# Reordering one queue's transfers in a four-layer graph network: adjacency load first, next token loads between the way out and the reads back

## The reference

```python
h = relu(layernorm(x)); x = x + L0(h, adj)          # 2-layer graph network, softmax masked by adj
h = relu(layernorm(x)); x = x + L1(h, adj, adj)     # 12-head attention, adj as bias
h = relu(layernorm(x)); x = x + L2(h, adj)          # 12-head attention, adj as bias
h = relu(layernorm(x)); x = x + L3(h, adj)          # 2-layer graph network:
    u = h @ h.T / sqrt(D); a = softmax(u) * adj; attn = a / (sum(a) + 1e-10)
    ctx = (attn*upper) @ (h @ wl.T) + diag(attn) * (h @ ws.T) + (attn*lower) @ (h @ wr.T)
    h = relu((ctx - mean) / sqrt(var + eps) * g + beta)
```

## Time and profile before

| | us |
|---|---|
| median of 3 runs | 2807.22 (2806.8 to 2807.78) |
| the profiled execution | 2810.98 |
| its span, first to last instruction | 2809.2 |
| PE busy in the span | 2684.6 (96%) |
| DVE, POOL, ACT busy | 2184.4, 1495.1, 1224.2 |
| mean granted TensorE clock | 0.988 |

### The profile page before, as it was taken

The page is one execution under the profiler, slowest core; times in us unless marked ns, Lnnn a source line. Parts: engine busy times, 40 slices in busy tenths (PEclk is TensorE's granted clock), DMA queues, the critical chain, the costliest instruction groups (busy, mean ns, idle before and its releaser), DMA issues.

```text
span 2809.2 us, 85451 instructions
## 1 busy us (share of the span) xinstructions
PE 2684.6 (96%) x33582; PEld 2472.3 (88%) x33582; DVE 2184.4 (78%) x4130; ACT 1224.2 (44%) x2007; POOL 1495.1 (53%) x2499
## 2 busy tenths in 40 slices
PE   7999999999988999999989999998999999999997
PEld 7988888888878899999888999998888888888886
DVE  5776777767767788888877888888677777777776
ACT  3333333333333454544544545454444444444443
POOL 2222222223214566665544666665677777777776
PEclk9999999999999999999999999999999999999999
DMA  5332232322323433333353333333132222222221
GB/s 162 103 108 84 84 106 63 113 77 89 103 76 108 142 121 124 125 123 121 108 158 111 121 122 127 121 122 119 55 96 80 71 90 78 71 90 78 72 84 48
DMA packets 224451, 284.59 MB, mean 101 GB/s; under 512 B 18256, under 2 KB 203984, under 8 KB 224336
## 3 DMA queue, kind: packets, MB, share of 16 engines
q1 hardware_dynamic: 224336, 282.96, 32.1%
HBM read 182.62 MB, written 100.27 MB: 101 GB/s over the span
## 4 chain that ended last, share of the span: by engine, by line
PE 37%; issue 22%; DVE 16%; POOL 15%; DMA 5%; ACT 3%; SPq 2%; POOLq 0%; DVEq 0%; ACTq 0%
PE ps L373 27%; POOL wide L1610 7%; PE ps L1435 3%; PE ps L1417 3%; PE ps L1450 2%; DMA adjin<-in_adj 2%; DVE heads L1308 2%; DVE wide L1299 2%; DVE heads L1316 2%; DVE heads L1322 2%; DMA bounce<-xin 1%; POOL small L722 1%; DVE wide L1332 1%; POOL wide L1595 1%; PE ps L1965 1%
## 5 line engine op out<-in xcount | busy, mean ns | idle before, releaser
L373 PE MATMUL ps<-w_hi,split 128*128 128x384 f32 x4608 | 1271.6, 346 | 26.3 <-ACT split L1673 17.6
L373 PEld LDWEIGHTS ps<-w_hi,split 128*128 128x128 f32 x4608 | 849.1, 191 | 56.9 <-issue 17.8
L373 PE MATMUL ps<-split,w_hi 128*128 128x256 f32 x4608 | 863.4, 283 | 14.8 <-DVE w_lo L450 11.1
L373 PE MATMUL ps<-w_lo,split 128*128 128x384 f32 x2304 | 787.6, 342 | 0.0
L373 PEld LDWEIGHTS ps<-split,w_hi 128*128 128x128 f32 x4608 | 721.3, 189 | 32.2 <-ACT w_hi L439 11.3
L373 PE MATMUL ps<-split,w_lo 128*128 128x256 f32 x2304 | 584.7, 283 | 0.0
L373 PEld LDWEIGHTS ps<-split,w_lo 128*128 128x128 f32 x2304 | 435.7, 189 | 17.3 <-issue 17.3
L373 PEld LDWEIGHTS ps<-w_lo,split 128*128 128x128 f32 x2304 | 439.0, 191 | 1.3 <-issue 1.2
L731 POOL TENSOR_TENSOR rstd<-mv,pos_half 128x2 f32<-128x2 f32 x64 | 59.0, 923 | 569.3 <-DVE mv L926 569.3
L1187 POOL TENSOR_TENSOR wide<-wide 128x192 f32<-128x192 f32 x256 | 213.4, 865 | 252.1 <-ACT wide L1253 252.1
L1610 POOL TENSOR_TENSOR wide<-wide,row 128x192 f32<-128x192 f32 x512 | 315.7, 652 | 1.5 <-ACT wide L1686 1.5
(11 more groups left out here) (145 smaller groups left out, 4473.8 us busy)
## 6 DMA issues: line engine op xcount, KB each, us to landing
bounce<-xin SPq DMA_DIRECT2D x127, 384.0 KB, 3.1
wide<-bounce SPq DMA_DIRECT2D x508, 96.0 KB, 2.2
x_after<-wide SPq DMA_DIRECT2D x96, 384.0 KB, 2.5
wide<-x_after SPq DMA_DIRECT2D x96, 384.0 KB, 3.3
xin<-x_after SPq DMA_DIRECT2D x190, 192.0 KB
xin<-in_x SPq DMA_DIRECT2D x66, 192.0 KB
wide<-in_x SPq DMA_DIRECT2D x32, 384.0 KB, 4.4
out<-wide SPq DMA_DIRECT2D x32, 384.0 KB, 2.8
```

The lines of the kernel that those rows point to most:

```text
L373: mm = nc.tensor.matmul(out, t if tokens_stay else w, w if tokens_stay else t, start=(k == 0), stop=(k == len(pairs) - 1))
```

## The change

`swap_quarters` is cut in two: `put_quarters` (wait for the turned group, write it to `bounce`) and `get_quarters` (wait until it has landed, four reads). In `turn(i)` the adjacency load comes before the way out, and the next token loads between the way out and the reads. No other engine's instructions change in kind or in order.

```diff
+    def at_turn(i):
+
         if isinstance(i, int) and i >= ITER:
-            if nxt == len(phases):
-                return
-            now, i = phases[nxt], i - ITER
+            return (phases[nxt] if nxt < len(phases) else None), i - ITER
+        return ph, i
+
+    def put_quarters(s, i):
+        now, i = at_turn(i)
+        if now is None:
+            return
         sp.wait_ge(now.dve_done[s], now.DV[s]("turned", i))
         sp.dma_start(g.bounce[s], g.turned[s][:]).then_inc(now.sems.bounced[s], 16)
+
+    def get_quarters(s, i):
+        now, i = at_turn(i)
+        if now is None:
+            return
         sp.wait_ge(now.sems.bounced[s], 16 * (i + 1))
...
     def turn(i):
         for s in range(STREAMS):
             store_and_reload(s, i - 2)
-            swap_quarters(s, i)
+            adjacency(s, i)
+            put_quarters(s, i)
             tokens(s, i + 1)
-            adjacency(s, i)
+            get_quarters(s, i)
```

More of the change, by code:

```diff
@@ L512, in tokens @@
             sp.dma_start(g.xin[s][:, t], source[i * STREAMS + s][t]).then_inc(now.sems.x_in[s], 16)
-    def swap_quarters(s, i):
-        now = ph
+    def at_turn(i):
         if isinstance(i, int) and i >= ITER:
-            if nxt == len(phases):
-                return
-            now, i = phases[nxt], i - ITER
+            return (phases[nxt] if nxt < len(phases) else None), i - ITER
[4 more added lines that the diff above has]
+            return
         sp.wait_ge(now.dve_done[s], now.DV[s]("turned", i))
         sp.dma_start(g.bounce[s], g.turned[s][:]).then_inc(now.sems.bounced[s], 16)
+    def get_quarters(s, i):
+        now, i = at_turn(i)
+        if now is None:
+            return
         sp.wait_ge(now.sems.bounced[s], 16 * (i + 1))
@@ L525, in swap_quarters @@
             sp.dma_start(now.bufs[s].hT0_rows[rows], g.bounce_quarter[s][k]).then_inc(now.sems.hT_in[s], 16)
+    def swap_quarters(s, i):
+        put_quarters(s, i)
+        get_quarters(s, i)
     def matrix(m):
```

## The result

The changed kernel takes 2837.8 us (median of four runs, 2835.6 to 2843.9) where the kernel before takes 2807.1: a ratio of 1.0112, with a 95% interval of 1.0095 to 1.013. It is 1.1% slower; I had forecast 0.8% faster. The profiled execution took 2835.6 us around a span of 2833.8; the one of before 2811.0 around 2809.2. That is 24.6 us more span.

The account below looks back on a forecast made before the run. PE bounds the kernel, except for its idle time in phase 3 (32.2 us, partly from late adjacency blocks) and at borders. Gains 10.8 + 5 + 2.7 + 2.7 + 1.5 = 22.7 us gave 2784.5 us; forecast 2775 to 2795, 8 in 10: 2773 to 2801.

Parts of the forecast that it names:

- Reads back later: Phase 3, stream 1: reads issued 1.56 us later land at 2224.5; DVE loses under 1 us, PE nothing.
- rival of late reads: Phase 3, stream 1: reads land behind the tokens, PE waits 0.65 us longer per turn, +9.1 us; 2813.9 us; chance 0.09.
- Adjacency load earlier, phase 3: Phase 3: block lands some 6 us earlier, POOL's 25 waits go; gains 10.8 us, plus 5 at L1772.
- the discount on L1772: Phase 3: only 5 us of PE's 7.3 us wait on DVE's L1772 counted, since DVE gets reads back later.
- the first rival: Phase 3: POOL's head start doesn't pay, PE keeps 15.8 us of gaps, only borders' 6.9 us gained; 2800.3 us; chance 0.14.
- PE's wait for ACT's split stays: Phase 3: PE's 12.8 us of waits on ACT's L1673 stay, since POOL itself waits on DVE in that chain.
- Late reads in phase 1 are hidden: Phases 0 and 1: use is 11.7 us behind the reads' start, so 3 to 5 us more are hidden.
- Adjacency at the borders: Borders to phases 1 and 2: 2.7 us gained together; border to phase 3: 1.5 us.
- Tokens earlier at the border to phase 1: Border of phases 0 and 1: tokens leave 1.35 us sooner twice, all of it counting; 2.7 us gained.
- the sum of 22.7 us: All gains, phase 3 and borders together: 10.8 + 5 + 2.7 + 2.7 + 1.5 us.

Follow-up runs that it names:

- number 9: Changed kernel, reads before tokens in: phase 3's stream 1 (0.9947); all phase 3 (0.9942); also phase 2's last two turns (0.9913); ratios to the kernel before.
- Number 1: Changed kernel with the four reads back right behind the way out again, tokens after them, adjacency load still early: 2777.9 us, ratio 0.9899.
- number 4: Changed kernel with each stream's tokens loaded by four DMAs of 32 rows instead of two of outer size 4: 2764.4 us, ratio 0.9845.
- number 7: Order of the kernel before (reads, tokens, adjacency last) with the tokens as four DMAs of 32 rows: 2775.2 us, ratio 0.9873.

## Why the prediction was wrong, point by point

- **Reads back later: the step that failed.** I had a lower bound of 2223.1 and an upper one of 2227.1 for the landing, took 2224.5 "nearer the lower bound since the reads' own row is the nearest kind", and gave the slower rival 0.09. The reads landed at 2228.0, beyond the upper bound. The row of 2.2 us is that of reads with nothing narrow ahead of them; it was not the nearest kind for reads behind tokens. The row that was, the 6.75 us that tokens took at the border, I had used for the bound and set aside. Even the bound that I made of it was 0.9 us too early. I also never asked why 384 KB of tokens need 6.75 us where reads of 96 KB, four in a row, land 2.2 us behind their issue: single microseconds of the trace of before show the tail at 0.26.
- **The rival of late reads** had the right mechanism and place (stream 1 of phase 3), and its price of the gaps was near. Its +9.1 us, with the 15.8 us not gained, are 24.9 us of gaps, 1.8 us a turn; 30.2 us were measured, 2.2 us a turn, or +10.9 us when the 19.3 us of gaps that went are taken off. The landing was 0.8 us later than its 2227.2, and PE stood ready sooner: in the turn shown only a landing by 2225.6 (2228.0 less PE's gap of 2.4) would have left no gap, where the rival decided at 2226.5. What it lacked is the clock at half rate behind nine of the gaps, 15 us. At the entry into phase 3 it counted 3 us; number 9 gives about 8. Its 2813.9 us became 2837.8.
- **Adjacency load earlier, phase 3: right.** The waits for adjacency and PE's waits for POOL and L1772 went. With reads first, where nothing hides it, the gaps lose 19.3 us, against 10.8 + 5 in my sum: the discount on L1772 was for late reads, and without them its wait goes but for 1.6 us at the end of the phase. POOL's head start does pay, so the first rival falls.
- **PE's wait for ACT's split stays,** right: 11.8 us in the changed kernel, 12.7 with reads first.
- **Late reads in phase 1 are hidden,** right: PE is busy 377.97 of 380 us with either kernel.
- **Adjacency at the borders.** With reads first, PE is busy 111.1 us at the border to phase 3 instead of 107.1, more than the 1.5 us counted. For the other two borders single profiles of one kernel differ by more than the 2.7 us (PE busy 154.8 and 151.3 us in 785 to 960 for reads first, run twice), so that term stays open.
- **Tokens earlier at the border to phase 1: wrong.** I let the landing follow the issue. It doesn't: the tokens left 1.6 us sooner and reached DVE at the same 802.8 to 802.9. That the reads behind them have a part on the same four engines would fit; no run takes it apart.
- **As a whole,** the sum of 22.7 us was made for a kernel whose reads land in time. Number 1 is such a kernel, but for the 2.7 us of earlier tokens, and it gains 1.0 to 1.1%, some 29 us, where the rest of the sum is 20.0. Gaps of phase 3 and its entry explain about 6 of the 9 us more; the others aren't traced. What I mis-weighed was one transfer's landing, and it outweighed all the rest.

What stays open: how the rest of about 0.0025 spreads over phases 0 to 2, and which of the gaps in PE lower the clock (the gap of 2.42 us before 2723.96 us left it at 1.00, the one of 1.96 us before 2616.62 us did not).

## What to carry to other kernels

Before a transfer is moved ahead of another, look at the DMA share of single microseconds while it runs: here a long stretch at a small constant share, 0.26, meant that it lay on a few engines, and what was issued behind it came late though it was spread itself. A load with a small outer size is worth cutting another way (here four loads of 32 rows instead of two of 4 x 32) before any order is tuned around it. And a late input of an engine that feeds PE can cost more than its wait, since the clock may fall behind the gap, as it did here in nine of 14 turns: price it with the clock, and give the upper bound of a landing the weight of the row it came from.

## What the runs showed of the hardware that I had not expected

- Two loads of 192 KB with an outer size of 4 move at some 97 GB/s, at a DMA share of 0.26; the same 384 KB in four loads of outer size 32 pass with shares of 0.68 to 0.75 at 191 to 211 GB/s, reads among them.
- Transfers behind such a load are late even if they are spread themselves: with 384 KB on four engines ahead DVE waited 3.8 us a turn, with 192 KB 1.6 us, with 16 KB not at all, and with 384 KB spread over all engines once in 2010 to 2745 us, 1.6 us.
- Single gaps of 2.0 to 2.6 us in PE, one a turn, brought the clock to 1.2 GHz for some 3.4 us behind them in nine of 14 turns; the five of the other turns, 1.5 to 2.4 us, did not. In the kernel before, gaps of at most 1.2 us, 32 us in all over 735, left it at 2.4 GHz.
- SP itself seems to be held up by narrow loads: at the start of the kernel it came to the first residual load at 15.15 us in the kernel before and at 11.84 us with spread tokens (number 4; 12.05 in number 7), though it had issued four more DMAs by then. No run takes this apart.
